# Depthwise chunks as half-precision pairs: the first image left out, its tap packing moved

## What is computed

```
def _L0_conv_ref(x, ln_w, ln_b, q_w, q_dw, kv_w, kv_dw, proj_w, temperature):
    b, c, h, w = x.shape
    xn = _layernorm_c(x, ln_w, ln_b)
    q = _dwconv3x3(_conv1x1(xn, q_w), q_dw)
    kv = _dwconv3x3(_conv1x1(xn, kv_w), kv_dw)
    k, v = jnp.split(kv, 2, axis=1)
...
    q = _l2norm(q)
    k = _l2norm(k)
    attn = jnp.einsum('bhcn,bhdn->bhcd', q, k) * temperature[None]
    attn = jax.nn.softmax(attn, axis=-1)
    out = jnp.einsum('bhcd,bhdn->bhcn', attn, v)
    out = out.reshape(b, c, h, w)
    return _conv1x1(out, proj_w)
...
x = x + _L0_conv_ref(_gn(x), ...)
x = x + _L1_conv_ref(_gn(x), ...)
```

## Time and profile before

| What | Value |
|---|---|
| time, median of 3 runs | 1691.7 us (1690.54 to 1692.43) |
| the profiled execution | 1687.0 us, its span 1685.2 us |
| PE busy | 1616.8 us (96%) |
| PEld busy | 1533.5 us (91%) |
| DVE busy | 1502.3 us (89%) |
| ACT busy | 1087.0 us (64%) |
| POOL busy | 591.3 us (35%) |
| granted TensorE clock, mean share of full speed | 0.973 |

### The profile page before, as it was taken

One profiled execution on the slowest core, in us unless ns is written; L12 is line 12 of the kernel. 1 busy time (PEld: TensorE's weight loads), 2 busy tenths in 40 slices (PEclk: granted clock), 3 DMA queues, 4 the chain that ended last, 5 costly groups with the idle time before them and its releaser, 6 DMA issues.

```text
span 1685.2 us, 38420 instructions
## 1 busy us (share of the span) xinstructions
PE 1616.8 (96%) x13789; PEld 1533.5 (91%) x13789; DVE 1502.3 (89%) x1979; ACT 1087.0 (64%) x1721; POOL 591.3 (35%) x400
## 2 busy tenths in 40 slices
PE   6979999999999998999999999899999999999998
PEld 5878968999999995999999997799999999689998
DVE  6799979999889968999978995999988997799996
ACT  4858777545476968665447896755536697765651
POOL 4899960232263003123228001122326500312232
PEclk9999988999999997999999999899999999799999
DMA  7002213766511210566640220366661021055563
GB/s 194 0 24 67 61 32 88 179 172 180 147 47 42 78 34 17 149 174 174 177 124 0 76 75 1 84 158 172 176 177 47 29 77 47 4 132 141 137 152 99
DMA packets 105039, 166.32 MB, mean 99 GB/s; under 512 B 40266, under 2 KB 78763, under 8 KB 104780
## 3 DMA queue, kind: packets, MB, share of 16 engines
q1 hardware_dynamic: 81772, 138.95, 32.5%
q10 hardware_dynamic: 23168, 26.04, 5.0%
HBM read 52.20 MB, written 25.17 MB: 46 GB/s over the span
## 4 chain that ended last, share of the span: by engine, by line
PE 74%; DVE 9%; issue 5%; ACT 3%; SPq 1%; DMA 1%; DVEq 0%; ACTq 0%
PE ps L998 40%; PE ps L850 15%; PE ps L825 9%; PE ps L855 5%; PE ps L883 3%; DVE region L1486 2%; DVE region L1764 1%; PE ps L993 1%; ACT region L1234 1%; ACT region L1165 1%; ACT region L1190 1%; DVE region L1761 1%; DVE region L1789 0%; ACT region L1215 0%; DVE region L1737 0%
## 5 line engine op out<-in xcount | busy, mean ns | idle before, releaser
L998 PE MATMUL ps<-region,W 128*96 128x256 f16 (+2 forms) x7140 | 792.0, 271 | 14.4 <-DMA region<-region 7.3
L998 PEld LDWEIGHTS ps<-region,W 128*96 128x96 f16 (+1 forms) x7140 | 780.7, 123 | 18.0 <-issue 8.5
L850 PE MATMUL ps<-region 128*128 (+2 forms) x2448 | 284.6, 277 | 16.7 <-DVE region L1486 12.6
L850 PEld LDWEIGHTS ps<-region 128*128 128x128 f32 x2448 | 278.1, 193 | 21.2 <-issue 16.6
L1234 ACT ACTIVATE region<-region 96x1584 f16<-96x1584 f32 (+2 forms) x80 | 98.4, 1272 | 285.7 <-DVE region L1698 285.7
L1486 DVE TENSOR_TENSOR region<-V,band_eps 128x2322 int32<-128x2322 int32 (+2 forms) x104 | 254.9, 2460 | 14.8 <-issue 7.7
L729 POOL TENSOR_TENSOR region<-region 96x528 f32<-96x528 f32 (+1 forms) x72 | 96.4, 1343 | 439.9 <-ACT region L1215 224.8
L825 PE MATMUL ps<-proj,region 96*128 96x240 f32 x1024 | 210.1, 368 | 2.4 <-DVE region L1458 1.9
L825 PEld LDWEIGHTS ps<-proj,region 96*128 96x128 f32 x1024 | 195.4, 191 | 16.0 <-DVE region L1458 2.3
L668 POOL TENSOR_TENSOR region<-region,cbias 128x576 f32 (+1 forms) x124 | 175.6, 1417 | 56.7 <-DVE region L1458 53.2
L719 POOL TENSOR_TENSOR region<-region,X 96x1536 f32<-96x1536 f32 x40 | 116.0, 2901 | 189.7 <-DVE region L1819 189.7
(11 more groups left out here) (244 smaller groups left out, 2138.5 us busy)
## 6 DMA issues: line engine op xcount, KB each, us to landing
region<-region SPq DMA_DIRECT2D x104, 247.5 KB, 4.2
region<-in_x_dram SPq DMA_DIRECT2D x128, 192.0 KB, 2.4
out_dram<-region SPq DMA_DIRECT2D x40, 576.0 KB, 4.3
region<-region ACTq DMA_DIRECT2D x72, 247.5 KB, 2.5
X<-in_x_dram SPq DMA_DIRECT2D x30, 576.0 KB, 6.2
region<-region SPq DMA_DIRECT2D x32, 247.4 KB, 5.1
X<-in_x_dram SPq DMA_DIRECT2D x19, 384.0 KB, 10.2
region<-region SPq DMA_DIRECT2D x24, 185.6 KB, 4.0
```

Source lines behind the costliest of these rows:

```text
L850: last = mm(o[:, to], T[:, i, 3 * c + d, 0:W], src[:, of], start=k == 0, stop=k == 2)
L998: last = mm(o, w, src, start=opens and k == 0, stop=k == len(steps) - 1, skip_group_check=g in (2, 4) or split and ck > 0)
```

## The change

In the first image all 24 chunks are now computed in float32: PE's `depthwise`, ACT's rounding and high halves and DVE's low halves take their split way only where b is above 0, and the counts that they wait for begin with the second image. `packed_taps()` stands in the first image behind the last strip and the two steps of `affine`, ahead of DVE's wait for the copy of the query-key sums. The three setup steps that make `QINV` and `QSC` stand at the end of the setup. The numbers in the second line count setup steps and are three lower for it.

```diff
@@ -357,7 +357,7 @@
         s_wt = plain_sem("weights_placed")
 
         NLOADS = 13
-        N_BOUND, N_RES, N_QKS, N_AMAX, N_WSC = 6, 9, 21, 26, 29
+        N_BOUND, N_RES, N_QKS, N_AMAX, N_WSC = 6, 9, 18, 23, 26
         N_COPIES = 4
         N_TURNED = 3 * (3 + 2) + 1
         N_SPLIT = 13 + NRT * 6 + 2
@@ -836,7 +836,7 @@
                     pe.wait_ge(s_qd, b * DK + n - 3 + START)
                     pe.wait_ge(s_qkl, b * 2 * GROUPS_QK + n - 3 + START)
                     if split is not None:
-                        pe.wait_ge(s_qs, b * NS + split + 1 + START)
+                        pe.wait_ge(s_qs, (b - 1) * NS + split + 1 + START)
                     ready = 0
                     for c in range(DC):
                         if c in (0, 1, 3):
@@ -857,10 +857,10 @@
                     last.then_inc(s_dw, 1)
 
                 for n in range(4):
-                    depthwise(n, n, 0 if n == 3 else None)
+                    depthwise(n, n, 0 if n == 3 and b else None)
                 with pe.Fori(0, 2) as k8:
                     for at in range(8):
-                        depthwise(k8 * 8 + 4 + at, at, k8 * 3 + 1 + (1, 4, 7).index(at) if at in (1, 4, 7) else None)
+                        depthwise(k8 * 8 + 4 + at, at, k8 * 3 + 1 + (1, 4, 7).index(at) if at in (1, 4, 7) and b else None)
                 for n in range(20, DK):
                     depthwise(n, n)
 
@@ -1130,21 +1130,21 @@
                     act.wait_ge(s_pq, (b + 1) * AT + START)
                     act.wait_ge(s_out, b * UNITS * 16 + START)
                     act.wait_ge(s_packed, 3 * len(SPLIT_RUNS))
-                    act.wait_ge(s_qs, b * NS + SPLIT.index(m) + START)
+                    act.wait_ge(s_qs, (b - 1) * NS + SPLIT.index(m) + START)
                     act.activation(rounded, words(m), ACT.Copy, scale=col(QSC, P)).then_inc(s_qh, 1)
 
                 def high_halves(m):
 
-                    act.wait_ge(s_ql, b * NS + SPLIT.index(m) + 1 + START)
+                    act.wait_ge(s_ql, (b - 1) * NS + SPLIT.index(m) + 1 + START)
                     act.activation(Q16[:, m * DC:(m + 1) * DC, :, HIGH].rearrange("p c h -> p (c h)"), rounded,
                                    ACT.Copy).then_inc(s_qs, 1)
 
                 for n in range(DK):
                     k2, i = divmod(n, 2)
                     evict(k2, i, k2 % 2, n >= 2 * GROUPS_QK)
-                    if n + AHEAD - 1 in SPLIT:
+                    if b and n + AHEAD - 1 in SPLIT:
                         high_halves(n + AHEAD - 1)
-                    if n + AHEAD in SPLIT:
+                    if b and n + AHEAD in SPLIT:
                         rounded_chunk(n + AHEAD)
                     for j in ((0,) if i == 0 else (1, 2)):
                         c = k2 * 3 + j
@@ -1362,9 +1362,6 @@
             link(setup, v.tensor_reduce(col(BMAX, P), cbias[:], AX.X, ALU.max, apply_absolute_value=True))
             link(setup, v.scalar_tensor_tensor(col(BMAX, P), ps[:, 3, CO:CO + 1], 10.0, col(BMAX, P), ALU.mult, ALU.add))
             link(setup, v.tensor_scalar(col(QINV, P), col(BMAX, P), 1e-30, None, ALU.max))
-            link(setup, v.tensor_scalar(col(QINV, P).bitcast(i32), col(QINV, P).bitcast(i32), 0x7F800000, None, ALU.bitwise_and))
-            link(setup, v.tensor_scalar(col(QINV, P), col(QINV, P), 2.0 ** -7, None, ALU.mult))
-            link(setup, v.reciprocal(col(QSC, P), col(QINV, P)))
             link(setup, v.tensor_scalar(col(BMAX, P), col(BMAX, P), col(TMAX, P), 1e-10, ALU.mult, ALU.max))
             link(setup, v.tensor_scalar(col(BMAX, P).bitcast(i32), col(BMAX, P).bitcast(i32), 0x7F800000, None, ALU.bitwise_and))
             link(setup, v.reciprocal(col(QKS, P), col(BMAX, P)))
@@ -1432,6 +1429,9 @@
                 link(setup, v.tensor_scalar(col(at), col(POW), factor / (WTOP * YSCALE), None, ALU.mult))
             link(setup, v.tensor_tensor(col(CLAMP, P), col(QKS, P), col(QKS, P), ALU.mult))
             link(setup, v.tensor_scalar(col(CLAMP, P), col(CLAMP, P), 1e-24, None, ALU.mult))
+            link(setup, v.tensor_scalar(col(QINV, P).bitcast(i32), col(QINV, P).bitcast(i32), 0x7F800000, None, ALU.bitwise_and))
+            link(setup, v.tensor_scalar(col(QINV, P), col(QINV, P), 2.0 ** -7, None, ALU.mult))
+            link(setup, v.reciprocal(col(QSC, P), col(QINV, P)))
 
             for b in range(B):
                 sv = N_PRE + b * NST
@@ -1477,7 +1477,7 @@
                     dve.wait_ge(s_out, b * UNITS * 16 + START)
                     dve.wait_ge(s_pq, (b + 1) * AT + START)
                     dve.wait_ge(s_V, N_TURNED)
-                    if n in SPLIT:
+                    if b and n in SPLIT:
                         dve.wait_ge(s_packed, 3 * len(SPLIT_RUNS))
                     mask = band[:].bitcast(i32).rearrange("p (i j) -> p i j", j=3).unsqueeze(1)
                     for c, channels in parts:
@@ -1517,19 +1517,17 @@
 
                 def low_halves(m):
 
-                    dve.wait_ge(s_qh, b * NS + SPLIT.index(m) + 1 + START)
+                    dve.wait_ge(s_qh, (b - 1) * NS + SPLIT.index(m) + 1 + START)
                     v.scalar_tensor_tensor(Q16[:, m * DC:(m + 1) * DC, :, LOW].rearrange("p c h -> p (c h)"),
                                            Q[:, m * DC:(m + 1) * DC, :].rearrange("p c h -> p (c h)"), col(QSC, P), rounded,
                                            ALU.mult, ALU.subtract).then_inc(s_ql, 1)
                 WHOLE = ((0, DC),)
                 bands(0, PARTS_OF_T)
                 bands(1, WHOLE)
-                if b < 1:
-                    packed_taps()
                 for n in range(2 * GROUPS_QK):
                     bands(n + 2, WHOLE)
                     low_parts(n)
-                    if n + AHEAD in SPLIT:
+                    if b and n + AHEAD in SPLIT:
                         low_halves(n + AHEAD)
                 for n in range(2 * GROUPS_QK + 2, DK):
                     bands(n, WHOLE)
@@ -1559,6 +1557,8 @@
                     strip(k)
                 affine(st, b * 3 + 2)
                 assert st.n == N_AFFN
+                if b < 1:
+                    packed_taps()
 
 
                 dve.wait_ge(s_pad, b + 1 + START)
```

## The result

The changed kernel takes 1679.7 us, the median of 5 runs (1678.41 to 1681.45), beside 1690.74 us for the kernel before (5 runs, 1686.37 to 1692.43): a ratio of 0.9937 [0.992, 0.9953]. In a second comparison unchanged copies took 1678.21 us (5 runs) and 1687.36 us (21 runs), 0.9944 [0.993, 0.9957]. So the change makes the kernel 9 to 11 us faster. The prediction was 1685.7 us with a range from 1681.0: the direction was right, the gain larger than the 6.0 us forecast, and the time lies 1.3 us under the range.

The account below looks back on a forecast made before the run. PE was taken to set the depthwise stage's pace, losing time in the first image to DVE's packing and small waits. Terms -11.5 + 5.3 + 0.2 = -6.0 us took the 1691.7 median to 1685.7 us; range 1681.0 to 1690.5.

Parts of the forecast that it names:

- I take the difference of the sum over to the median unchanged.: Whole kernel: the -6.0 us worked out on the profiled execution (1687.0 us timed) was applied to the 1691.7 us median.
- the stage: First image's depthwise convolution, seven more chunks in full precision: ends at 201.4, -11.5 us with the setup's 0.6 included.
- the packing's term: Behind the first image's strips: 8.2 us of packing less 2.93 us of wait, +5.3 us, bounds +0.5 to +11.0.
- The setup: Three links leave DVE's setup chain, so the first image starts earlier: -0.6 us, bounds 0 to -0.6.
- the clock: Ahead of the first attention products: the granted clock may fall sooner while DVE packs, +0.2 us, bounds 0 to +0.6.
- chunk 2 would be quick without the idle time: First image's depthwise stage: chunk 2 starts at about 110.9 instead of 119.92, with no reason for its 5.86 us.
- 22 chunks need 4.07 us each: First image's depthwise stage: 22 full-precision chunks from chunk 2 on take 89.5 us on PE.
- PE's waits are near 1 us: First image's depthwise stage: PE's waits for band matrices were given 1.0 us, between 0 and 3.
- that rival: First image's depthwise stage: DVE becomes the bound, from 3.45 us per band matrix on; +12.4 us, 1704.1 us, chance 0.06.
- POOL's end: POOL's weight split in the first image: estimated to end between 218 and 226, so the packing again runs beside POOL.
- the prediction's second rival: Packing behind the strips: all three runs go like the first, 13.9 us; gain given back, -0.5 us, 1691.2 us, chance 0.14.
- the 200 to 203 that I gave: Sign in the changed profile: the first image's query-key products should begin at 200 to 203 us.

Follow-up runs that it names:

- short course: Traced executions of the unchanged kernel before with 110.2 to 110.5 us from first depthwise chunk to first query-key product; they took 1687.0 and 1687.11 us.
- long course: Traced executions of the unchanged kernel before with 114.7 to 115.0 us from first depthwise chunk to first query-key product; 1688.51, 1692.11 and 1691.27 us.
- long copy 1: The kernel before, unchanged, run again for a second trace: 1688.51 us, with 114.71 us from first depthwise chunk to first query-key product.
- copy 1 of the changed one: The changed kernel, unchanged, run again for a second trace and more times: ratio 0.9944 to the kernel before.

## Why the prediction came out too high

*The steps that failed* are two. The first is the sentence "I take the difference of the sum over to the median unchanged." The sum was made against an execution of 1687.0 us, and 1687.0 - 6.0 = 1681.0. That execution was one of the short course. The median of 1691.7 us came from three runs of 1690.54 to 1692.43 us, near the times of two executions of the long course (1691.27 and 1692.11 us). Those three have no trace, so that they were long ones is inferred from their time; and time alone doesn't decide it, since the long copy 1 took 1688.51 us, and 21 later runs had a median of 1687.36 us. The changed kernel takes away what sets the two courses apart, so it gains more from the long one. The difference belonged to one execution, the level to others. In the stage that is 2.5 us: -13.45 by the means of the traces, where -10.9 was forecast.

The second is the packing's term, +5.3 us: by the means it was +2.75, 2.5 us less. The setup's and the clock's terms erred the other way by 2.3 us together, so -8.8 us came of the -6.0.

Against the execution that I read, the span came out at 1679.7 us where 1685.2 - 6.0 = 1679.2 was forecast. That is partly luck. There the packing's term was 2 us too high and the first chunk came 1.9 us later than forecast; and the traced execution, at 1681.45 us, was the slowest of the changed kernel's five.

*The stage.* Without the setup's 0.6 us I had -10.9; beside the short course it is 99.56 - 110.47 = -10.9, beside the long one -15.1 to -15.4. That chunk 2 would be quick without the idle time, that 22 chunks need 4.07 us each, that PE's waits are near 1 us: these hold (0.30 + 0.29 us of waits, 94.62 us for 23 chunks, 4.11 each). DVE did not become the bound: 72.44 us for 24 chunks are 3.0 us per band matrix, under the 3.45 from which that rival decides.

*The packing* was mis-sized. It cost 18.2 - 15.0 = +3.2 us beside the short course and +2.4 beside the long one, not +5.3, within the bounds. Two things differ from the working: DVE reaches it 10.7 us behind the first query-key product, not 12.0, so that the wait it fills is 14.97 - 10.67 = 4.3 us, not 2.93; and it takes 7.55 us, not 8.2. POOL's end at 220.5 lies in the stretch that I gave (218 to 226). The first run is again the odd one (3.89 us), the others are near the clean ones.

The Trainium skill's page "SBUF — State Buffer" (Who interferes with whom) states that a VectorE instruction with two SBUF inputs contends with a GpSimd instruction that reads SBUF, and not with one that only writes it. The trace agrees that they slow each other: 5.22 us for the packing without POOL, 9.17 and 7.55 us beside it. That each of the nine two-input steps would wait for POOL, as the prediction's second rival has it, is not borne out. In the changed kernel the second and third group of three such steps took 0.66 and 0.65 us, as without POOL (0.66), and they stood beside POOL's memset (218.56 to 220.50), which only writes; so these two do not speak against the page. In the kernel before, beside steps of POOL that read, they took 0.74 and 1.37 us.

*The clock.* From the sums to the convolution it is 0.6 us more in two traces of the changed kernel and 1.2 in one (36.8 and 37.4 against 36.2 us). I had +0.2 for the clock, up to 0.6. Nearly all of it stands ahead of the first addition to x (L1602), in DVE's waits for PE. The kernel before, then copy 1 of the changed one:

```profile
232.27 0.26 DVE L1593 COPY region<-ps 128x96 f32<-128x96 f32 x1 [0.62 <-PE ps L908]
...
234.10 1.22 DVE L1602 SCALAR_TENSOR_TENSOR X<-ps,X 96x1024 f32 x1 [1.57 <-PE ps L918]
```

```profile
225.74 0.26 DVE L1593 COPY region<-ps 128x96 f32<-128x96 f32 x1 [0.90 <-PE ps L908]
...
228.39 1.22 DVE L1602 SCALAR_TENSOR_TENSOR X<-ps,X 96x1024 f32 x1 [2.39 <-PE ps L918]
```

From the first step on the sums to L1602 these are 6.26 and 7.45 us; in the other two traces of the changed kernel 6.86 and 6.82. Over the first 4 us of this stretch the granted clock is 1.00 before, and 0.76, 0.50 and 0.74 in the three traces after, where PE had stood idle for 3.8 us while DVE packed and began on the sums, and PE's products of L908 took 0.74 us in place of 0.46. So this is the clock, and its term was too small: 0.6 to 1.2 us.

*The setup* gave nothing that can be told from the spread; I had -0.6 with zero as the other bound. The first chunk came at 103.73, not at 101.8, and so the query-key products at 203.29, just outside the 200 to 203 that I gave.

*The whole.* With the means of the five and three traces in the table: stage -13.45, to the sums +2.75, to the convolution +0.79, behind it +0.06; the first chunk itself is 1.08 us later in these three, 0.6 us of it because the loads of x came later. Together -8.8 us; timed, 1678.21 - 1687.36 = -9.2 us.

*What stays open:* what decides which course an execution of before takes. All five show the short stage with the lower clock at 56 to 58 us and the long one without it, and the changed kernel has both clocks there and one stage. Whether the slow chunk 2 itself leads to the other meetings of DVE and POOL, or goes with them, is open as well; in the one trace of the kernel before without POOL beside it, neither is there.

## What to carry to other kernels

Before a difference worked out from one trace is put on a median, look whether that trace's time lies where the median does; where they differ by much of the expected gain (here 4.7 us against 6.0), the kernel may have several courses, and the change may act on one of them more. A chain of many small VectorE steps belongs where PE has work queued and GpSimd is silent, not merely where VectorE waits: the packing cost over 8 us ahead of chunk 2, about 3 us behind the strips and nothing that shows in the convolution. With GpSimd silent it cost nothing behind the strips either (14.78 us to the sums, against 14.97 before the change).

## What was not expected of the hardware

- An idle time of 8.33 us on PE cost more than itself: the granted clock fell to 0.50 during it, and stayed there for 3.4 us of work in one execution and 5.6 us in another, so the next chunk took 5.86 or 6.93 us in place of 4.25. After an idle time of 3.46 us the chunk took 4.26 us.
- Single-input steps were slowed beside POOL as well: three L1499 steps of 128 x 18 took 0.51 us without POOL and 1.01 us with it, three copies of L1506 0.34 and 1.24 us. With the packing in the convolution the step L1576 took 1.03 us in place of 0.24 and ended with POOL's memset. But three L1499 steps of 128 x 54 took 0.62 us both beside that memset and without POOL; what tells the cases apart stays open.
- Without POOL a band matrix took 2.56 to 2.58 us each time. Beside it, it took up to 4.06 us, and the kernel before then differed by 4.4 us from one execution to another in this stage alone.
